# Local attention's masked keys: 128 transfers an iteration into zeroed buffers in place of GpSimd products, and one set of padded values in place of two

## What is computed

```python
qkv = hidden_states @ w_qkv.T + b_qkv          # 16 heads x 16 features, for q, k and v
# groups of 64, split in halves of 32: attention inside every half
scores = einsum('bghqd,bghkd->bghqk', q, k) / head_dim ** 0.5
w = softmax(scores, axis=-1)
out = einsum('bghqk,bghkd->bghqd', w, v)
out = out.transpose(0, 2, 1, 3, 4).reshape(b, n, h * d)   # a fixed regrouping of the output
```

## Time and profile before

| What | Value |
|---|---|
| median of 3 runs | 9148.5 us (9129.78 to 9150.74) |
| the profiled execution: its own time, its span | 9143.53 us, 9141.9 us |
| mean granted TensorE clock | 0.924 of full speed |
| busy: PE, DVE, ACT, POOL | 85%, 79%, 68%, 30% |
| local attention of the first iteration, from the first zeroing to the next norm | 120.75 us |

### The profile page before, as it was taken

One profiled execution on the slowest core, in us unless ns is written; L12 is line 12 of the kernel. 1 busy time (PEld: TensorE's weight loads), 2 busy tenths in 40 slices (PEclk: granted clock), 3 DMA queues, 4 the chain that ended last, 5 costly groups with the idle time before them and its releaser, 6 DMA issues. The chain is left out here.

```text
span 9141.9 us, 163324 instructions
## 1 busy us (share of the span) xinstructions
PE 7776.9 (85%) x65408; PEld 2851.3 (31%) x65408; DVE 7227.1 (79%) x9490; ACT 6201.5 (68%) x11410; POOL 2700.3 (30%) x3046
## 2 busy tenths in 40 slices
PE   6799877998779987799877998779977799777997
PEld 3222342223422234222342223422234222342223
DVE  5899558995589955899558995589955899558995
ACT  4499544995449954499544995449955499554995
POOL 3233241332413324133241332413324133241322
PEclk9899987999879998799988999889999799897998
DMA  0100001000010000100001000010000100001000
GB/s 28 42 23 23 10 10 42 23 23 10 10 42 23 23 12 9 42 23 23 14 7 45 23 20 16 5 46 23 19 17 4 46 23 19 19 1 46 23 19 19
DMA packets 216827, 204.98 MB, mean 22 GB/s; under 512 B 105783, under 2 KB 141111, under 8 KB 216055
## 3 DMA queue, kind: packets, MB, share of 16 engines
q1 hardware_dynamic: 216060, 194.46, 7.4%
HBM read 123.83 MB, written 67.37 MB: 21 GB/s over the span
## 5 line engine op out<-in xcount | busy, mean ns | idle before, releaser
L1257 DVE TENSOR_REDUCE mfull<-ps 128x1 f32<-128x1024 f32 x4096 | 4692.9, 1217 | 225.1 <-PE ps L1181 220.7
L1339 ACT ACTIVATE work<-ps 128x512 f32<-128x512 f32 x8192 | 4385.6, 597 | 346.9 <-PE ps L1203 225.0
L1221 PE MATMUL ps<-work,vbuf 128*32 128x256 f32 x32768 | 2623.2, 392 | 116.6 <-ACT hh L1359 116.6
L1181 PE MATMUL ps<-kop,qop 48*128 48x512 bf16 x8192 | 2507.2, 394 | 59.1 <-DVE mfull L1257 51.7
L1203 PE MATMUL ps<-qop,kop 51*128 51x512 bf16 x8192 | 2489.2, 384 | 0.0
L1221 PEld LDWEIGHTS ps<-work,vbuf 128*32 128x32 f32 x32768 | 654.3, 108 | 1800.9 <-issue 896.0
L1203 PEld LDWEIGHTS ps<-qop,kop 51*128 51x128 bf16 x8192 | 482.2, 93 | 1649.6 <-ACT work L1339 1585.9
L1287 POOL CAST mpart<-mfull 128x32 bf16<-128x32 f32 x128 | 27.0, 211 | 2541.6 <-DVE mfull L1257 2363.6
L1305 POOL TENSOR_TENSOR work<-work,none 128x16 f32<-128x16 f32 x128 | 371.7, 2904 | 1014.4 <-ACT work L1348 1014.4
L263 PE MATMUL ps<-ident,hh 128*128 128x128 f32 x1024 | 200.0, 373 | 510.4 <-DVE hh L233 510.4
L416 POOL TENSOR_TENSOR hh<-work,hmask 128x1024 f32<-128x1024 f32 x256 | 522.1, 2065 | 129.7 <-PE ps L344 129.6
(11 more groups left out here) (163 smaller groups left out, 9125.6 us busy)
## 6 DMA issues: line engine op xcount, KB each, us to landing
qop<-scratch SPq DMA_DIRECT2D x512, 64.0 KB
scratch<-work SPq DMA_DIRECT2D x32, 768.0 KB, 3.6
scratch<-hh SPq DMA_DIRECT2D x32, 768.0 KB, 4.6
kop<-scratch SPq DMA_DIRECT2D x256, 96.0 KB
vbuf<-in_x SPq DMA_DIRECT2D x9, 2048.0 KB, 8.3
qop<-scratch SPq DMA_DIRECT2D x512, 32.0 KB
kop<-scratch SPq DMA_DIRECT2D x256, 64.0 KB
out<-x SPq DMA_DIRECT2D x64, 256.0 KB, 2.1
```

What stands on the lines that cost most here:

```text
L1181: pe.matmul(ps[:, b + n, :], qop[r:r + KQ, s, i, t * P:(t + 1) * P], kop[r:r + KQ, s, i, half(n)], start=True, stop=True).then_inc(s_ms, 1)
L1221: mm = pe.matmul(ps[VW * i:VW * (i + 1), OB, cols], vp[:, b, t, (G * gl + i) // 2, :], prob[:, u % PS, i, cols], start=t == 0 and part == ...
L1257: v.tensor_reduce(mfull[:, g % 2, r // ROWS, i * T + t:i * T + t + 1], ps[:, b:b + NB, :].rearrange("p b n -> p (b n)"), AX.X, ALU.max).th ...
L1339: act.activation(prob[:, u % PS, hl, :], ps[:, EB[slot % len(EB)], :], ACT.Exp, scale=scale).then_inc(s_ex, 1)
```

## The change

The masked keys are no longer products. Two buffers of 4096 float32 columns each (`cleared`: one where the four kx were, one where the second sequence's padded values were) are zeroed once an iteration by POOL. SP then requests, for every pair of tiles and both chunks, one transfer for each of 8 heads: 16 partitions x 256 keys, from qkT into the head's place in the buffer, 16 KB each. That is 16 transfers a pair and 128 an iteration. The rest of the buffer stays zero, since a head's partitions and columns are the same for every pair. A pair's transfers raise one semaphore of the buffer by 256 in all; scores(t) waits for it, and SP waits, before it fills a buffer again, for the scores of the pair that used it.

There is one set of padded values instead of two, and both sequences use it. The second sequence's v_piece(1, r) moves from slots 4, 5, 6, 7 to slots 4, 6, 8, 10, and v_keep(1, r) from slots 5, 6, 7, 8 to slots 5, 7, 9, 11, where it waits for values(2r + 1), the last reader of the part that it overwrites. values(8), (10), (12) and (14) wait for their own v_keep.

```diff
--- before.py
+++ after.py
@@ -276,12 +276,15 @@
 
             qkT = work[:, 0:8 * N].rearrange("p (b m n) -> p b m n", b=PB, m=4)
 
-            zeroed = work[:, 8 * N:16 * N].rearrange("p (b k) -> p b k", b=PB)
-            vz = work[:, 8 * N:16 * N].rearrange("p (b t h w) -> p b t h w", b=PB, t=T, w=2 * LD)
-            vze = work[:, 8 * N:16 * N].rearrange("p (t j e s d) -> p t j e s d", t=TT, e=2, s=2, d=LD)
+            padded = work[:, 8 * N:12 * N]
+            vz = padded.rearrange("p (t h w) -> p t h w", t=T, w=2 * LD)
+            vze = padded.rearrange("p (t j e s d) -> p t j e s d", t=T, e=2, s=2, d=LD)
 
             PT = [low[:, 2 * N * i:2 * N * (i + 1)].rearrange("p (h n) -> p h n", h=LH) for i in range(2)]
-            kx = [hh[:, i * N:(i + 1) * N].rearrange("p (h n) -> p h n", h=LC) for i in range(4)]
+            cleared = [hh[:, 0:4 * N], work[:, 12 * N:16 * N]]
+            kx = [y.rearrange("p (c h n) -> p c h n", c=C, h=LC) for y in cleared]
+            PAIR = 2 * P
+            KXS = 16 * C * LC
             sd = [qf[:, i * HALF:(i + 1) * HALF].rearrange("p (h n) -> p h n", h=LH) for i in range(2)]
             pr = [qf[:, (2 + i) * HALF:(3 + i) * HALF].rearrange("p (h n) -> p h n", h=LH) for i in range(2)]
             o = 16 * N
@@ -296,7 +299,8 @@
             VB = 4
             KV = (2, 3, 0, 1)
             VR = T // 2
-            s_kx, s_sc, s_mx, s_sd = sem("la_kx"), sem("la_sc"), sem("la_mx"), sem("la_sd")
+            s_kx = [sem(f"la_kx{i}") for i in range(2)]
+            s_sc, s_mx, s_sd = sem("la_sc"), sem("la_mx"), sem("la_sd")
             s_pr, s_zs, s_rz, s_nm = sem("la_pr"), sem("la_zs"), sem("la_rz"), sem("la_nm")
             s_tr, s_pa, s_o, s_x = sem("la_tr"), sem("la_pa"), sem("la_o"), sem("la_x")
             s_rg, s_xs = sem("la_rg"), sem("la_xs")
@@ -337,21 +341,23 @@
                             pe.wait_ge(s_qke, len(KV) * (b + 1))
                         if t >= 2:
                             pe.wait_ge(s_sd, t - 1)
+                        pe.wait_ge(s_kx[t // 2 % 2], KXS * (t // 4 + 1))
                         for c in range(C):
-                            pe.wait_ge(s_kx, C * t + c + 1)
                             for k in range(BLK):
                                 r = slice(k * LB, (k + 1) * LB)
                                 mm = pe.matmul(ps[r, t % 2, c * 256:(c + 1) * 256],
                                                qkT[:, b, c, tb * P + k * LB:tb * P + (k + 1) * LB],
-                                               kx[(C * t + c) % len(kx)][:, :, r],
+                                               kx[t // 2 % 2][:, c, :, t % 2 * P + k * LB:t % 2 * P + (k + 1) * LB],
                                                start=True, stop=True)
                             mm.then_inc(s_sc, 1)
 
                     def values(t):
                         b, tb = t // T, t % T
                         pe.wait_ge(s_pa, BLK * (t + 1))
-                        if tb == 0:
-                            pe.wait_ge(s_vz, VR * (b + 1))
+                        if b == 0 and tb == 0:
+                            pe.wait_ge(s_vz, VR)
+                        if b and tb % 2 == 0:
+                            pe.wait_ge(s_vz, VR + tb // 2 + 1)
                         if t >= 2:
                             pe.wait_ge(s_x, t - 1)
                         for c in range(C):
@@ -359,7 +365,7 @@
                                 for j in range(4):
                                     i = LC * c + 2 * j + e
                                     mm = pe.matmul(ps[32 * j:32 * (j + 1), 2 + t % 2, c * P:(c + 1) * P],
-                                                   vz[:, b, tb, i, :], PT[t % 2][:, i, :], start=e == 0, stop=e == 1,
+                                                   vz[:, tb, i, :], PT[t % 2][:, i, :], start=e == 0, stop=e == 1,
                                                    skip_group_check=True)
                         mm.then_inc(s_o, 1)
 
@@ -391,8 +397,8 @@
                             values(t - 2)
                         if t < 4:
                             qk_piece(1, t)
-                        elif t < 8:
-                            v_piece(1, t - 4)
+                        elif t < 4 + 2 * VR and t % 2 == 0:
+                            v_piece(1, t // 2 - 2)
                         if REGROUP <= t < REGROUP + 4:
                             regroup(0, t - REGROUP)
                     for k in range(4):
@@ -400,35 +406,42 @@
 
                 @block.gpsimd
                 def _(pool):
-                    for b in range(PB):
-                        pool.memset(zeroed[:, b, :], 0.0).then_inc(s_z, 1)
+                    pool.memset(cleared[0], 0.0).then_inc(s_z, 1)
+                    pool.memset(padded, 0.0).then_inc(s_z, 1)
+                    pool.memset(cleared[1], 0.0).then_inc(s_z, 1)
                     for i in range(2):
                         pool.memset(PT[i], 0.0).then_inc(s_z, 1)
-                    for t in range(TT):
-                        b, tb = t // T, t % T
-                        if tb == 0:
-                            pool.wait_ge(s_qke, len(KV) * b + 2)
+
+                @block.sync
+                def _(sp):
+                    for j in range(TT // 2):
+                        b, at = j // (T // 2), j % (T // 2) * PAIR
+                        if j % (T // 2) == 0:
+                            sp.wait_ge(s_qke, len(KV) * b + 2)
+                        if j < 2:
+                            sp.wait_ge(s_z, (1, 3)[j])
+                        else:
+                            sp.wait_ge(s_sc, 2 * C * (j - 1))
                         for c in range(C):
-
-                            i = C * t + c
-                            if i >= len(kx):
-                                pool.wait_ge(s_sc, i - len(kx) + 1)
-                            pool.tensor_tensor(kx[i % len(kx)],
-                                               qkT[:, b, 2 + c, tb * P:(tb + 1) * P][:, None, :].to_broadcast([P, LC, P]),
-                                               hmask[:, :, None].to_broadcast([P, LC, P]), ALU.mult).then_inc(s_kx, 1)
+                            for i in range(LC):
+                                r = slice(LD * i, LD * (i + 1))
+                                sp.dma_start(kx[j % 2][r, c, i, :],
+                                             qkT[r, b, 2 + c, at:at + PAIR]).then_inc(s_kx[j % 2], 16)
 
                 @block.vector
                 def _(v):
                     bias = b_v[:, :].rearrange("p (j e d) -> p j e d", e=2, d=LD)
 
                     def v_keep(b, r):
-                        if r == 0:
-                            v.wait_ge(s_z, b + 1)
+                        if b == 0 and r == 0:
+                            v.wait_ge(s_z, 2)
+                        if b:
+                            v.wait_ge(s_o, 2 * r + 2)
                         v.wait_ge(s_val, VR * b + r + 1)
                         src = ps[:, VB + r, :].rearrange("p (t j e d) -> p t j e d", t=2, e=2, d=LD)
                         for i in range(2):
                             for e in range(2):
-                                ins = v.tensor_tensor(vze[:, T * b + 2 * r + i, :, e, e, :], src[:, i, :, e, :],
+                                ins = v.tensor_tensor(vze[:, 2 * r + i, :, e, e, :], src[:, i, :, e, :],
                                                       bias[:, :, e, :], ALU.add)
                         ins.then_inc(s_vz, 1)
 
@@ -486,8 +499,8 @@
                             shift(t)
                         if t >= 1:
                             turn(t - 1)
-                        if 5 <= t < 9:
-                            v_keep(1, t - 5)
+                        if 5 <= t < 5 + 2 * VR and t % 2:
+                            v_keep(1, (t - 5) // 2)
                         if REGROUP < t <= REGROUP + 4:
                             residual(0, t - REGROUP - 1)
                     for k in range(4):
@@ -512,7 +525,7 @@
                         if t >= 2:
                             act.wait_ge(s_o, t - 1)
                         else:
-                            act.wait_ge(s_z, PB + t + 1)
+                            act.wait_ge(s_z, t + 4)
                         for k in range(BLK):
                             r = slice(k * LB, (k + 1) * LB)
                             act.copy(PT[t % 2][r, :, r], pr[t % 2][r]).then_inc(s_pa, 1)
```

## The result

| | before | after |
|---|---|---|
| median of 6 runs each (range), us | 9145.2 (9129.8 to 9152.2) | 9193.6 (9182.2 to 9201.4) |
| profiled execution: own time, span, us | 9143.5, 9141.9 | 9193.9, 9192.2 |
| mean granted clock | 0.924 | 0.919 |
| local attention, mean of 8 iterations, us | 122.28 | 127.72 |

The ratio is 1.0052, with a 95% interval of 1.0039 to 1.0065: 48 us slower, more than the 0.3% that a measurement can tell. The last row of the table goes to the norm's power on POOL, which is seen in every iteration; it ends 1.45 us after the point that the 120.75 us go to. The expectations of the first four experiments use the shorter measure (120.8 before, 126.3 after), those of the others the longer. 127.72 - 122.28 = 5.44 us an iteration, 43.5 in eight, is most of the 50.3 us by which the spans differ.

A forecast was written before the change was run, and what follows sets the result against it. Bound: local attention's TensorE chain from odd tile to odd tile, waiting for ScalarE's placing, without key products. Turns -0.3 plus one clock fall 3.4 give +3.1 us an iteration, +24.8 in 8, on 9148.5: 9173 us; range 9130 to 9225.

The forecast's parts named there:

- one fall an iteration, as before: Local attention's turns: TensorE's clock falls once an iteration, inside a chain with a v piece; +3.4 us, chance 0.37.
- the rival of two falls: Local attention, turns 2 and 3 become alike: two clock falls, +6.5 us an iteration, 9200 us; chance 0.14.
- the transfers: SP's key requests: 0.37 us each, a pair requested in 6.0 us, hidden by the turn; cost 0.
- a sign of being wrong: Local attention: TensorE's scores waiting for keys, with SP's requests over 0.55 us, would show the forecast wrong.
- that of the keys: Rival, keys late: SP bounds the turn; at 0.735 us a request +12 us an iteration, 9245 us; chance 0.12.
- The chain: Local attention, odd tile's scores to next odd tile's: turns 1 to 3 each 9.95 us, turns 4 and 5 10.1.
- The price of a fall: Half-clock work in a turn's chain: values 0.86, scores 0.94, v piece 1.59, together 3.4 us a fall.
- the -0.3 of my sum: Five odd turns, tile 5 to 15, without the fall term: 50.05 us against 50.35, 0.3 us less an iteration.
- Landing: Key transfers: 2.1 us from issue to landing, so a pair has landed after 8.1 us.
- GpSimd's part: Local attention: removing POOL's products saves 0 of TensorE's wait; DVE's multiplication shortens 0.04 us a turn, to 0.68.
- Even tiles: Rival: the even chain, losing both v pieces, sets the end; tile 15 3.8 us earlier, 9118 us; chance 0.08.
- The zeroing and the added waits: POOL's three fills end at 58.8 us, before the first placing; v_keep's and values' new waits already met; 0 each.

The follow-up runs named there:

- first four experiments: The follow-up runs e1, e2, e3 and e4, with medians of 9162.5, 9196.9, 9186.9 and 9199.8 us.
- e5: e2 plus eight further unread products on TensorE between scores and values in slots 6, 8 and 10; 9155.0 us, ratio 1.0002.
- e2: The changed kernel with one request for both chunks of a head, 8 requests a pair instead of 16; 9196.9 us, ratio 1.0069.
- e4: The changed kernel with its 16 key transfers a pair read from DRAM, where other data lie; 9199.8 us, one run.
- e3: The changed kernel with 2 key requests a pair instead of 16 from an iteration's third pair on; 9186.9 us, one run.
- e7: e2 with the second sequence's v pieces ahead of the values in their slots; 9093.2 us, ratio 0.994.
- e6: The changed kernel, 16 requests a pair, with the second sequence's v pieces ahead of the values in their slots; 9173.4 us, one run.
- e9: e1 with the second sequence's v pieces ahead of the values in their slots; 9146.3 us, ratio 1.0004.
- e1: The kernel before with only the v pieces and v_keep moved to the new slots, POOL's products kept; 9162.5 us, ratio 1.003.

## Why the prediction was right or wrong

The time, 9194 us, lies in the range, and "slower" was the likeliest sign by a little. But 9173 missed by 20 us, and two steps failed. The first is the one about the clock: "I take one fall an iteration, as before". There are three, in seven of the eight iterations one in each of the turns 1 to 3. I had seen that such a wait "now comes in each of two or three turns" and even that turns 2 and 3 become alike (the rival of two falls, 9200 us), and still counted one. The second is the transfers, at 0.37 us a request, of which I wrote "I take 0": a request costs 0.63 to 0.70 us, SP sets the pace, and scores wait 52.6 us for keys, which I had named as a sign of being wrong. Each of the two alone gives about the measured time, and they do not add up since they run side by side. That the time fell into the range is in part luck: had the rival of two falls (+52 us) and that of the keys (+50 by its own working, below) added up, it would have been some 9250 us.

- **The chain.** 9.95 us for turns 1 to 3 at full clock: e5 has 9.95 and 9.95. 10.1 for turns 4 and 5: 10.05 and 10.01.
- **The price of a fall.** 3.4 us was too much for one. In e2, where no keys are waited for, the three turns of the first iteration exceed 9.95 by 1.63, 2.63 and 1.77 us. A fall hits values and v piece there, seldom the following odd scores, and often only part of them. With these 6.0 us, the -0.3 of my sum makes +5.7, which is near the measured +5.44 an iteration. So the term is three falls of some 2 us, not one of 3.4. In after the three turns exceed 9.95 by 1.31, 0.75 and 2.34 us, but SP's pace holds them as well. My reading of the rows was wrong in one place, too: 6.3 us of work in a turn is not less than in both turns that kept the clock, since one of them had 5.95.
- **The requests.** 0.37 us was wrong; it is 0.63 to 0.70, near the upper bound of 0.735 that I had. My reason for the lower row, as many partitions and long pieces, did not hold: those 8 requests read from DRAM, and e4 shows that the source matters (420 against 589 ns). By the condition that I set, 0.62 us each, SP had to bound the turn, and it does. By my working of that rival, with 11.1 us a pair, the last keys would land at 53.2 + 8 x 11.1 + 1.8 = 143.8 and scores(15) start some 4 us later, at 147.8 for 141.6: +6.2 us, x 8 = +50, 9198 us. That is nearly the measured time; in the trace scores(15) start at 146.10. I gave this rival 0.12. e2 and e3 do not rule it out: they show that the falls hold the stage where the keys no longer do.
- **Landing.** 1.8 us, where I took 2.1. Transfers do not wait for each other: 16 go out in 11.1 us. The Trainium skill ("DMA: Bandwidth & Descriptors", Rules for kernel authors) wants many small ones made into one, and here two chunks in one request cost SP the 593 ns of one, which agrees; it pays where SP is the only bound (e7 against e6) and not where the falls stand beside it (after against e2). The 2 us that the prediction took from the Trainium skill ("DMA: Bandwidth & Descriptors", Anatomy of one DMA — SWDGE (gpsimd) path) stand there for transfers issued from GpSimd; these are issued from SP.
- **GpSimd's part.** In before its products were off the path, as the waits had said. The multiplication at 0.68 in every tile holds (693 ns at most). The Trainium skill ("SBUF — State Buffer", Who interferes with whom) has a DVE instruction with two inputs in SBUF contend with a GpSimd instruction that reads SBUF; the 2232 ns before, 693 after and 2351 in e9 agree, though in e1, with the products kept, the longest was 817, so it needs more than the products' presence.
- **Even tiles.** False: nothing came earlier for the freed even chains.
- **The zeroing and the added waits.** No wait for any of them shows in the first iteration's stage.

On what a wait costs: in e2 the wait of 4.20 us is followed by half speed; in e5, with 0.55 us of wait left, the clock stays at 1.00. In the first iteration of after waits of 2.0 to 2.2 us for keys stand in each of the three turns with a fall. The Trainium skill ("TensorE: Matmul & The Clock Gate", HAM oscillation — how this bites in real kernels) describes a kernel that loses the clock in each wait for its data, anew every time, and advises an order that keeps TensorE at work; e2 and e5 agree, though ScalarE is waited for there and not a transfer, while in e7 every second turn keeps the clock with a wait of like length.

Left open: by the medians e1 has 26 us of the 48 and e2 61, while the profiled stages of both are as long as that of after; where their other executions differ was not found. That SP's requests alone would hold after at its length is read from its rows and from e6; no run takes the falls out of after and leaves its requests. Of the 50 us between the spans some 7 lie outside local attention, where the code is the same. e3, e4 and e6 have one time each, so of them only the stage is read.

## What to carry to other kernels

When work is moved in an in-order list, look at which side of the engine's wait it lands: behind the wait it lengthened the chain (9.95 us a turn), ahead of it it was hidden in the wait (7.9 us, or 9.5 with a clock fall, e7), and fewer turns had such a fall. Allow for a clock fall in each long wait, and price it at most by the half-clock length of what stands right behind it. And when a run takes away a wait that the profile names, here 52.6 us for keys, and gets no faster, the wait is not cleared by that: a second bound may stand beside it. See in the trace which queue never pauses, and take both away.

## What was not expected of the hardware

- A request between two places on the chip occupied SP for 589 ns (median), one from DRAM with as many partitions for 420 ns, and 16 or 32 KB made no difference (589 and 593).
- Added work made a kernel faster: e5 does 3.7 us more products in each of three turns than e2, and is 0.7% faster against before (1.0002 for 1.0069).
- The multiplications of over 2 us went away in e1 too (817 ns at most), though POOL multiplied as before, and came back in e9 (2351 ns), where only the v pieces' place differs from e1.
